# Last scatters awaited by SyncE, gates stored from the tile they are made in, and the router's logits moved into the attention's block

## The reference, cut to what matters

```python
x = _layernorm(x + _L0_attn_ref(x, w_in, w_out))                  # 16 heads, causal, ALiBi
x = _layernorm(x + _L0_xattn_ref(x, ctx_1024, ctx_1024, ...))     # 16 heads
x = _layernorm(x + _L0_ffn_ref(x, Wr, br, W1, b1, W2, b2))

# inside _L0_ffn_ref
probs = jax.nn.softmax(x @ Wr + br, axis=-1)      # logits: [8192, 8]
gates, ids = jax.lax.top_k(probs, K)              # K = 2
...
h = jax.nn.silu(jnp.einsum('ecd,edh->ech', xg, W1) + b1[:, None, :])
out = jnp.einsum('ech,ehd->ecd', h, W2) + b2[:, None, :]
y = jnp.zeros((N, Dm), x.dtype).at[disp_tok].add(out * disp_g)
```

## Time and profile before

| What | us |
|---|---|
| Median of 3 runs (lowest and highest) | 1586.39 (1585.27 to 1587.44) |
| The profiled execution's own time | 1587.09 |
| Its span, first to last instruction | 1585.4 |
| Attention block ends (release of its barrier) | 924.0 |
| Logits block ends | 965.4 |
| Routing block ends | 1070.9 |
| TensorE busy over the span | 1424.7 (90%) |

### The profile page before, as it was taken

How to read it: one execution, slowest core, us unless ns; L and a number is a source line. 1 busy time by engine, 2 the same in 40 slices (tenths; PEclk the granted TensorE clock), 3 DMA queues, 4 the chain that set the end, 5 groups by cost and what they waited for, 6 DMA issues and landing times. The chain is left out here.

```text
span 1585.4 us, 43757 instructions
## 1 busy us (share of the span) xinstructions
PE 1424.7 (90%) x17886; PEld 1198.1 (76%) x17886; DVE 1019.1 (64%) x2266; ACT 990.9 (63%) x1456; POOL 619.9 (39%) x688
## 2 busy tenths in 40 slices
PE   7999999999999999999999773158999999999990
PEld 5777777777777777777777652048999999999980
DVE  5666666666677777777777647884454454454582
ACT  4677777777777677777767554205565565565563
POOL 2644444454452322222232100013455455455485
PEclk9999999999999999999999976558999999999995
DMA  6021222122221222222221174003443443443464
GB/s 195 22 62 62 62 62 61 44 61 62 62 62 57 82 66 82 82 82 82 74 79 43 58 212 102 0 11 101 97 105 48 99 102 49 100 103 50 97 240 180
DMA packets 115142, 130.72 MB, mean 82 GB/s; under 512 B 26650, under 2 KB 97084, under 8 KB 114944
## 3 DMA queue, kind: packets, MB, share of 16 engines
q1 hardware_dynamic: 100288, 106.18, 21.5%
q0 software_dynamic: 14656, 21.74, 7.9%
HBM read 83.73 MB, written 44.16 MB: 81 GB/s over the span
## 5 line engine op out<-in xcount | busy, mean ns | idle before, releaser
L527 ACT ACTIVATE at_pr<-at_A 128x2048 f32<-128x2048 f32 x128 | 240.8, 1881 | 145.5 <-PE at_A L347 145.5
L622 DVE TENSOR_REDUCE at_mx<-at_A 128x12 f32<-128x1536 f32 x128 | 224.7, 1755 | 57.6 <-PE at_A L312 54.0
L767 POOL TENSOR_SCALAR_AFFINE_SELECT at_pr<-at_pr 128x2048 f32<-128x2048 f32 x64 | 128.6, 2010 | 204.9 <-ACT at_pr L527 204.8
L1839 POOL DMA_INDIRECT total<-ex_o,ids x70 | 115.8, 1654 | 187.5 <-DVE ex_o L1767 172.5
L1708 DVE TENSOR_TENSOR ex_hT<-ex_h,ex_hT 128x384 fp32r<-128x384 f32 (+1 forms) x192 | 113.0, 589 | 98.9 <-ACT ex_hT L1641 84.9
L658 DVE TENSOR_TENSOR at_oT<-at_C,at_oT 128x512 fp32r<-128x512 f32 x64 | 44.3, 692 | 164.9 <-ACT at_oT L540 164.9
L347 PE MATMUL at_A<-at_qp,at_kt 32*128 32x256 f32 x2048 | 139.8, 388 | 0.0
L362 PE MATMUL at_C<-at_pr,at_v 128*32 128x128 f32 x4096 | 138.3, 276 | 1.0 <-ACT at_oq L534 1.0
L1640 ACT ACTIVATE ex_h<-ex_U,ex_b 128x384 f32<-128x384 f32 (+1 forms) x192 | 116.3, 606 | 33.3 <-PE ex_U L35 27.4
L362 PEld LDWEIGHTS at_C<-at_pr,at_v 128*32 128x32 f32 x4096 | 104.0, 109 | 43.3 <-issue 42.1
L35 PE MATMUL ex_U<-ex_xT,ex_w_even 128*128 128x384 f32 (+1 forms) x576 | 115.3, 360 | 5.1 <-ACT ex_hT L1641 3.5
(11 more groups left out here) (245 smaller groups left out, 3067.9 us busy)
## 6 DMA issues: line engine op xcount, KB each, us to landing
ex_w_in<-in_w SPq DMA_DIRECT2D x16, 1024.0 KB
at_turned<-in_x_turned SPq DMA_DIRECT2D x16, 512.0 KB, 4.6
at_x<-in_x SPq DMA_DIRECT2D x16, 512.0 KB, 4.0
x<-at_y SPq DMA_DIRECT2D x32, 256.0 KB, 2.3
at_x<-x SPq DMA_DIRECT2D x16, 512.0 KB, 3.9
at_turned<-in_ctx_turned SPq DMA_DIRECT2D x16, 512.0 KB, 4.6
rows<-at_y SPq DMA_DIRECT2D x32, 256.0 KB, 2.2
total<-at_y SPq DMA_DIRECT2D x32, 256.0 KB, 3.1
```

What stands on the lines that cost most here:

```text
L527: nc.scalar.activation(pr[:, k % 2].rearrange("p i n a q -> p (i n a q)"), A[:].rearrange("p i n a q -> p (i n a q)"), ACT.Exp).then_inc(e ...
L622: nc.vector.tensor_reduce(mx[:, k % 2, 0:12], A[:, 0:3].rearrange("p i n a k -> p (i n a) k"), AX, ALU.max).then_inc(max_done, 1)
L767: nc.gpsimd.affine_select(out=t, in_=t, compare_op=ALU.is_ge, fill=0.0, base=0, pattern=[[0, 16], [1, P]], channel_multiplier=-1).then_inc ...
L1839: nc.gpsimd.indirect_dma_start(sum_dram, bass.IndirectOffsetOnAxis(ap=ids[0:n, e, at:at + 1], axis=0), o[0:n, pr, b, :], None, bounds_chec ...
```

## The change

Three edits.

**1. The logits lose their block.** `logits_block` becomes `logits_programs`, which returns pieces that each engine of the attention block calls in its tail. There is no barrier between attention and logits any more. The tiles are shared: the turned rows go to the attention's PSUM tile A (four banks), the logits and what is turned back to its banks B and C, and the casts to `sT`. SyncE issues `load_for_logits` one group earlier. `turn_rows(0)` and `turn_rows(1)` stand between the last steps of TensorE, with their casts and remainders on ScalarE and VectorE; the rest follows behind `output(63)` and `normalise(63)`. SyncE's loads of groups 4 and 5 are issued ahead of `store(63)`, those of groups 6 to 15 behind it.

**2. The gates are stored from `cand`.** The copy to `gate_rows` goes; SyncE writes `cand` itself, and VectorE waits for `gates_stored` before it writes `cand` again, after the search.

**3. The last scatters are awaited by SyncE.** `pool.wait_ge(own_stored, 16 * LT)` goes, and `sp.wait_ge(own_stored, 16 * LT)` stands at the end of SyncE's program of the block.

```diff
@@ attention_layers, SyncE
-                if g == groups - 1:
+                if g == groups - 2:
                     load_for_logits()
+            def load_later(i):
+                for u in (2 * (layer_groups + i), 2 * (layer_groups + i) + 1):
+                    sp.wait_ge(y_stored[u % 4], stored_before(u + 4))
+                load_rows(sp, i)
+
             store(halves_of - 2)
+            clear_rest(sp)
+            load_later(LOGIT_LOADS)
+            load_later(LOGIT_LOADS + 1)
             store(halves_of - 1)
+            for i in range(LOGIT_LOADS + 2, layer_groups):
+                load_later(i)
             for u in range(halves_of - 4, halves_of):
                 sp.wait_ge(y_stored[u % 4], stored_before(u + 4))
+            rest_cleared(sp)
@@ attention_layers, TensorE
             set_back(sets - 1)
+            turn_rows(pe, 0)
             output_back(halves_of - 1)
+            turn_rows(pe, 1)
             output(halves_of - 1)
+            tensor_program(pe, lambda engine: engine.wait_ge(res_done, halves_of))
@@ attention_layers, ScalarE
             copy_o(sets - 1)
+            copy_rows(act, 0)
             copy_out(halves_of - 1)
             normalise(halves_of - 2)
-            normalise(halves_of - 1)
+            copy_rows(act, 1)
+            scalar_program(act, lambda: normalise(halves_of - 1))
@@ attention_layers, VectorE
             normalise_set(sets - 2)
+            split_matrix(dve)
             residual(halves_of - 2)
             deviation(halves_of - 2)
             normalise_set(sets - 1)
+            rest_of_rows(dve, 0)
             rest_o(halves_of - 1)
+            rest_of_rows(dve, 1)
             residual(halves_of - 1)
             deviation(halves_of - 1)
+            vector_program(dve)
@@ logits_programs (new), the order of TensorE and ScalarE
+        pe.wait_ge(wr_ready, 1)
+        logits_of(0)
+        last_sum(pe)
+        for g in range(2, groups):
+            turn_rows(pe, g)
+            logits_of(g - 1)
+            back(g - 2)
...
+        add_bias(0)
+        last_normalise()
+        for g in range(2, groups):
+            copy_rows(act, g)
+            add_bias(g - 1)
+        add_bias(groups - 1)
@@ route_block
-            sp.dma_start(rows_dram[0:tiles * P, D:D + E].rearrange("(t p) e -> p t e", p=P), gate_rows[:]).then_inc(gates_stored, 16)
+            sp.dma_start(rows_dram[0:tiles * P, D:D + E].rearrange("(t p) e -> p t e", p=P), cand[:]).then_inc(gates_stored, 16)
...
-            link(v.tensor_tensor(cand[:], pr[:], eq[:], ALU.mult))
-            v.tensor_copy(gate_rows[:], cand[:]).then_inc(gates_made, 1)
+            v.tensor_tensor(cand[:], pr[:], eq[:], ALU.mult).then_inc(gates_made, 1)
+            dve.wait_ge(gates_made, 1)
...
+            dve.wait_ge(gates_stored, 16)
             for kth, chosen in enumerate((first, second)):
                 link(v.tensor_tensor(cand[:], chosen[:], st[:], ALU.mult))
@@ experts_block, SyncE and GpSimd
+            sp.wait_ge(own_stored, 16 * LT)
...
-            pool.wait_ge(own_stored, 16 * LT)
```

More of the change, by code:

```diff
@@ new lines, in rest_cleared, with turn_rows @@
+    def rest_cleared(sp):
+        sp.wait_ge(zeroed, 48)
+    def turn_rows(pe, g):
+        if g == 0:
+            pe.wait_ge(const_in, 48)
+        pe.wait_ge(x_loaded[g % LOADS], 16 * (g // LOADS + 1))
+        if g >= 2:
+            pe.wait_ge(d_copied, 2 * (g - 1))
+        for half in range(HALVES):
+            for n in range(NB):
+                last = nc.tensor.matmul(T[2 * (g % 2) + half][:, n * P:(n + 1) * P],
+                                        x2[:, g % LOADS, n, half * P:(half + 1) * P], ident[:],
+                                        start=True, stop=True, is_transpose=True)
+        last.then_inc(turned, 1)
@@ new lines, in tensor_program, with logits_of, back @@
+    def tensor_program(pe, last_sum):
+        def logits_of(g):
+            pe.wait_ge(a_copied, 2 * g + 2)
+            pe.wait_ge(d_copied, 2 * g + 2)
+            if g >= 2:
+                pe.wait_ge(l_done, g - 1)
+            for part in range(2):
+                for t in range(HALVES):
+                    last = nc.tensor.matmul(lb[g % 2], wr_s[:, t, :, :].rearrange("p a e -> p (a e)"),
+                                            xT[:, g % 2, part, t, :],
+                                            start=(part == 0 and t == 0), stop=(part == 1 and t == HALVES - 1))
+            last.then_inc(l_full, 1)
+        def back(g):
+            pe.wait_ge(l_done, g + 1)
+            if g >= 2:
+                pe.wait_ge(b_done, g - 1)
+            for n in range(NB):
+                last = nc.tensor.matmul(bb[g % 2][:, n, :, :].rearrange("p a e -> p (a e)"), lT[:, g % 2, n * P:(n + 1) * P],
+                                        ident[0:2 * E, 0:2 * E],
+                                        start=True, stop=True, is_transpose=True)
+            last.then_inc(b_full, 1)
+        pe.wait_ge(wr_ready, 1)
[5 more added lines that the diff above has]
+            back(g - 2)
+        logits_of(groups - 1)
+        back(groups - 2)
+        back(groups - 1)
@@ new lines, in copy_rows, with scalar_program, add_bias @@
+    def copy_rows(act, g):
+        if g == 0:
+            act.wait_ge(const_in, 48)
+        act.wait_ge(turned, g + 1)
+        if g >= 2:
+            act.wait_ge(l_full, g - 1)
+        for half in range(HALVES):
+            nc.scalar.copy(xT[:, g % 2, 0, half, :], T[2 * (g % 2) + half]).then_inc(a_copied, 1)
+    def scalar_program(act, last_normalise):
+        def add_bias(g):
+            act.wait_ge(l_full, g + 1)
+            if g >= 2:
+                act.wait_ge(b_full, g - 1)
+            nc.scalar.activation(lT[:, g % 2, :], lb[g % 2], ACT.Identity, bias=br[:, 0:1]).then_inc(l_done, 1)
+        add_bias(0)
[4 more added lines that the diff above has]
+        add_bias(groups - 1)
@@ new lines, in vector_program, with take @@
+    def vector_program(dve):
+        def take(g):
+            dve.wait_ge(b_full, g + 1)
+            nc.vector.tensor_reduce(logits[:, g * NB:(g + 1) * NB, :], bb[g % 2].rearrange("p n a e -> p n e a"),
+                                    AX, ALU.add).then_inc(b_done, 1)
+        for g in range(2, groups):
+            rest_of_rows(dve, g)
+            take(g - 2)
+        take(groups - 2)
+        take(groups - 1)
+    return load_rows, clear_rest, rest_cleared, turn_rows, tensor_program, copy_rows, scalar_program, split_matrix, rest_of_rows, vector_program
@@ L1924, in decoder_layer @@
                              {k: ins["attn_" + k] for k in ("wq", "wk", "wv", "wo")},
[L1925 to L1926 removed]
+                             {k: ins["xattn_" + k] for k in ("wq", "wk", "wv", "wo", "bq", "bk", "bv", "bo")}, ins, inputs, logits, iota8, rows)
         moe(nc, tokens, cap, ins, rows, total, out, logits, iota8)
```

155 lines of the change are left out of this document (41 added, 114 removed).

## The result

| | before | after |
|---|---|---|
| Median, us (lowest to highest, runs) | 1586.91 (1585.27 to 1587.77, 4) | 1576.2 (1573.49 to 1577.39, 4) |
| The profiled execution's own time | 1587.09 | 1573.49 |
| Its span | 1585.4 | 1571.7 |
| TensorE busy over the span | 1424.7 (90%) | 1422.2 (90%) |

After over before is 0.9933, 95% interval 0.9918 to 0.9948: 10.7 us less, between 8 and 13. For the median 1574.6 was predicted, between 1570.8 and 1578.0.

What follows compares the result with a forecast made beforehand. TensorE, busy 90% of the span, was taken as the bound, so gains lie where it idles. Joint 10.0, gates' copy 0.34 and kernel's end 1.5 sum to 11.8 us: 1574.6 us, range 1570.8 to 1578.0.

Steps and rivals of the forecast that it cites:

- The point that decides: Attention-to-logits joint: group 2's casts on ScalarE move from 930.86 to 920.7, right behind normalise(63), 10.2 us earlier.
- the 0.8: Joint: extra us won if the clock holds through output(63), limited by VectorE's remainders until 915.3; 11.0 us in all.
- The clock, the open part: Joint: added turns either hold TensorE's clock (11.0 us, 9.3 with a later fall) or don't (9.8 us).
- that branch's 9.3 us: Joint's gain if the clock holds through output(63), then falls in some 2.4 us of idleness, costing about 1.7 us.
- the 10.0 I took: Gain in us forecast for the attention-to-logits joint, chosen between 9.3 and 11.0.
- the branch of constant length: Kernel's end: GpSimd's DRAIN keeps its length and starts at 1578.6 in place of 1580.1, gaining 1.5 us.
- The short DRAIN: Rival at the kernel's end: DRAIN ends 2.0 us after the last record, gaining 4.6 us; 1571.5 us in all, chance 0.14.
- The sign named for it: Kernel's end: DRAIN starts about 0.1 us after the last scatter's record; length 5.0, 2.0 or 6.6 us tells the gain.
- Half given back: Rival in the logits: clock stays down for two stretches or loads 6 and 7 come late; 1579.5 us, chance 0.10.
- Nothing moves: Rival at the joint: group 2's casts still wait until about 931 for a late transfer or residual; 1586 us, chance 0.03.
- slower: Rival in the logits: row loads lose their lead, a group takes 5.0 us in place of 2.30; 1601 us, chance 0.03.
- theory K: Experiment's theory, kernel's end: DRAIN's fixed 4.2 us belongs to GpSimd's 147 earlier indirect transfers of the experts.

Runs made afterwards that it cites:

- Seven scatters: The changed kernel without the last scatters of the first three row tiles, seven of ten left; its DRAIN ended 4.76 us after the last scatter's record.
- casts first: The changed kernel with ScalarE's casts of group 2 ahead of normalise(63): 1573.17 us, ratio 0.9911 to the kernel before; on another chip 1567.09 us, 0.9907.

## Why the prediction was right, point by point

- **What bounds the joint.** The point that decides was named rightly: the casts of group 2 moved from 930.86 to 917.88. The earlier end of the attention in this trace is 902.91 - 901.27 = 1.64 us of the 13 us, so 11.3 us are the change's. 10.2 were forecast with 0.8 more if the clock held. The extra is `output(63)` at full clock, through which the layer norm's chain, and with it `normalise(63)`, ran 1.1 us sooner: the 0.8 was 0.3 us too small.
- **The clock, the open part.** Of the two branches the first came: the turns held the clock, TensorE then idled 2.31 us (2.4 forecast) and the clock fell there. Its cost was put at 1.7 us. The neighbouring rows show 1.77 - 1.09 = 0.7 for the logits and 1.71 - 1.09 = 0.6 for the turn, 0.2 for the small product, and the traces with and without the fall differ by 1.41 us of busy time: 0.3 us smaller than the term. With the 0.3 us above, that branch's 9.3 us became 9.84. That the 10.0 I took comes so near is partly luck: it is a middle value between branches, and no branch gave it. The price was also not one number: in two of eight traces with this joint the fall lasted about twice as long and cost 2.75 us of busy time (47.27 against 44.52), which gives 8.5 us for the joint.
- **Transposes and the clock.** A stretch of 3.46 us of turns alone, at half clock at its start, was followed by full clock at 919.87 with the turns moved behind, and with the turns in place 910 to 913 stood at 1.00. Both agree with the reading of the earlier trace rows; the plainest case is the earlier trace rows, where TensorE idles 8.67 us, then runs 16 transposes alone, at half clock at first, and behind them the logits' four matmuls take 1.10 us, their time at full clock:
```profile
928.85 1.10 PE L904 MATMUL lg_L<-lg_xT,lg_wr_s 128*16 128x512 f32 x4 [0.44 <-DVE lg_xT L969]
```
  The transposes here are f32 in transpose mode. The rule of the Trainium skill, "TensorE: Matmul & The Clock Gate", Part 4, that transposes don't count as busy in the same way, does not describe these traces.
- **turn_rows(0), turn_rows(1), split_matrix, the bias.** 1.04 us each for the turns, in gaps of 2.02 and 1.40 us; `residual(62)` still waited 0.19 us (0.72 in the earlier trace rows) for TensorE behind the three small instructions of `split_matrix`. All at no cost, as forecast.
- **Loads.** No load was waited for. The kernel with two loads behind the last store shows what cover they had: it lacked 1.65 us, inside the "at most 1 to 2 us" of the prediction, which left out the clock: it fell in that wait.
- **Edit 2.** 0.35 us, 0.34 forecast.
- **Edit 3.** 1.60 us, 1.5 forecast, on the branch of constant length. The short DRAIN, given 0.14, falls: the 2.0 us of the earlier trace rows don't carry over to the kernel's end. The lower bound of 0 falls too. The sign named for it did not show as described: the DRAIN's record starts not 0.1 us behind the last scatter but 8 us ahead of its end, and its length is 12.9 us. Only its end tells, 5.0 us behind the scatter.
- **The sum.** 11.8 forecast, 11.97 by the traces. The medians give 10.7 us with an interval of 8.3 to 13.0, which holds both. An execution with the longer fall would gain 8.52 + 0.35 + 1.60 + 0.18 = 10.65 us by these rows; how many of the untraced ones had it isn't known. The spans differ by 13.7 us, 1.64 of it the kernel's start.
- **The rivals.** "Half given back", 6.6 us at the joint and nothing at the end, is excluded by 9.84 us at the joint, a period of 2.3 us and the 1.60 us at the end. Its mechanism, a clock that stays down for two stretches, did come in the two traces with the longer fall, with 8.5 us left of the joint. "Nothing moves" and "slower" are excluded by the casts at 917.88 and by the absent waits for loads.

What stays open: why GpSimd's DRAIN has 4.18 us of its own at the kernel's end, and ends only 1.9 to 2.0 us after the last gather at the end of the routing (that gather's record is itself 2.40 us long). The runs show that it isn't the last scatters. Whether it is the 87 gathers and 70 scatters of the experts before them, as theory K has it, or something else of this block, wasn't tried.

## What to carry to other kernels

When a block boundary stands between a chain of waits and work that needs nothing of it, move pieces of that work into the chain's own gaps: it removes the boundary, and here the filled gaps held TensorE's clock as well. Then look for the next first wait: here an engine's fixed order put a layer norm's wait in front of casts whose input was ready, and swapping the two was worth another 3.2 us, half of it idle time and half the clock. Moving a wait off the engine whose closing DRAIN ends the kernel gave what the wait had lasted (1.6 us), and no more.

## What the runs showed of the hardware

- **The clock fell at places where the instructions don't differ.** Windows of 10 to 15 us, before the change and after it; the code there is the same:
```profile
10.00:15.00 5.00, 4.38 (x12) 3.45 (x13) 4.51 (x13) 1.27 (x2) 0.00 (x0) 0.66 1.08 386
```
```profile
10.00:15.00 5.00, 4.86 (x26) 3.36 (x30) 3.01 (x11) 2.00 (x4) 0.00 (x0) 1.00 1.06 377
```
  A second such place lies near 890 to 898. Of 14 traces four had neither fall, and the last softmax started at 901.2 to 901.7; eight had one of the two, 902.2 to 903.1; two had both, 903.9. The changed kernel itself had none in one trace (901.27) and the one in 10 to 15 us in the other (902.56), so it isn't the change's: some 1.4 us an execution for each, of which one would have been put down to the change had the spans been subtracted.
- **The fall in the new joint has two lengths.** From 920.0 it lasted until 923.4 in the change's trace, and the joint took 52.79 us; with no scatters at the end, where the joint's code is the same, it lasted from 921.1 to 927.9 and the joint took 54.11 us:
```profile
902.92:957.02 54.10, 47.27 (x360) 31.90 (x353) 29.39 (x67) 33.24 (x60) 2.74 (x9) 0.94 0.52 151
```
  Seven scatters gave 54.11 us as well, the six other traces of this joint 52.76 to 52.83. Without the wait of 2.31 us (casts first, two traces) there was no fall at this place. So the swap is worth 1.4 us of busy time against six of these traces and 2.7 us against two, which may be part of the 5.6 us by the medians on the second chip; that was not separated.
- **Chips differ in one stage.** From `runs` to the last scatter's record it was 598.8 to 600.2 us in the four traces of one chip and 594.2 to 594.5 us in three of another with all scatters, while the joint was the same (52.80 and 52.82 with edit 1). Ratios are taken within one chip only.
- **GpSimd's DRAIN at the end lasts 4.18 us with no transfer in flight**, and 0.083 us more for each indirect scatter issued right ahead of it.
